# Splitting the expert weights of a mixture layer ahead of the expert loop, during an attention

## The chip, the cores and the metric

One core of a Trainium2 chip runs the whole program. The metric is the device time of one execution, in microseconds (us). PE is TensorE, VectorE stands in the profile as DVE, ScalarE as ACT, GpSimd as POOL, and SP is SyncE, whose queue issues every DMA of this kernel.

## What is computed

Two blocks on a tensor x of 2 x 1024 tokens by 128 features. Each block adds an attention and a feed-forward part to x. Cut to what matters:

```python
# block 0: cosine attention, 16 heads of 8, over 1024 tokens; and an FFN with FP4 (blockwise) quantised x, weights, hidden
xn = layernorm(x)
x = x + attn0(xn) + ffn0(xn)
# block 1: linear attention, 4 heads of 32; and a mixture of 160 experts, top 8, hidden size 64
xn = layernorm(x)
x = x + attn1(xn) + moe(xn)

def moe(x):
    probs = sigmoid(x @ router_w.T + expert_bias)
    combine = top8_normalised(probs) * 2.5                  # [tokens, 160], zero for experts not chosen
    h1 = silu(einsum('th,eih->eti', x, w_gate))             # w_gate [160, 64, 128]
    h1w = h1 * combine.T[:, :, None]
    routed = einsum('eti,ehi->th', h1w, w_down)             # w_down [160, 128, 64]
    return routed + silu(x @ w_gate_shared.T) @ w_down_shared.T
```

All experts are computed for all tokens.

## The kernel before

The program is written engine by engine, in one block per engine; each engine runs its own list in order, and semaphores (`wait_ge`, `then_inc`) tie the lists together. So an instruction that waits holds up everything behind it on its engine.

**Attention of block 0.** It runs twice, once for each batch of 1024 tokens (`attention(0)`, some 54 to 183 us, and `attention(1)`, some 211 to 340 us). Each has 64 steps (`STEPS0`) in 8 groups (`GRP`) of 8 steps (`NB`). A step on PE is `scores(st, 0)`, then `values(st - 2)`, then `scores(st, 1)`. `scores` is two matmuls into two PSUM banks of 0 to 3; ScalarE turns each set into exponentials `E` (L418, one instruction of 128 x 1024 for each `u`), and `values` is eight recorded matmuls (L1045) into bank 4 or 5. `scores(st + 1, 0)` waits until the exponential of `scores(st, 0)` has been taken, since both use the same banks. At a group's end VectorE copies the result to `OS` (L741, in `output(m)`), PE transposes it (`out_T(m)`, L1054, four transposes, at step 4 of the next group) into bank 6 or 7 in turn, and VectorE divides it (`divide(m)`, L728 and L733).

Between these, VectorE does other work in the order of its list. In the first attention: `second_heads(2)`, `output(0)`, `second_heads(3)`, `output(1)`, `quantise_weights()`, `output(2)`, then `quantise_x(g)` and `output(3 + g)` for g of 0 to 3, then the last `output`. In the second: `quantise_hidden(g)` and `output(8 + g)` for g of 0 to 3, then `residual()`, then the last four `output`. A quantisation is ten VectorE instructions, L646 to L666; `residual()` is two, L772 and L774.

**Expert loop.** 160 experts make 80 pairs (`NP`); a pair fills the 128 partitions. Each pair has 4 steps (`NC`), one for every 512 tokens, 320 in all. Weights and activations are used as a high and a low part in fp32r, so that a product is three matmuls of 128 x 512. A step on PE is `down(s)` (L1342 to L1344), then `gate(s + 4)` (L1335 to L1337). For a gate, ScalarE applies silu (L562), VectorE multiplies by the combine rows `CWB` (`weigh`, L936), ScalarE rounds to the high part (`high`, L358), and VectorE subtracts for the low part (`low`, L941); then the down matmuls follow.

Once per pair the raw weights, 64 KB of gate (`wg_raw`, L208) and 64 KB of down (`wd_raw`, L211), loaded by SP, are transposed by PE in `weights_T` (L1314, L1317) ahead of the gate of the next step; ScalarE makes the high parts (`w_high`), VectorE the low parts (`w_low`, L926). SP's order in the loop, for each pair: wait `wg_pe`, load gate; wait `m_dve`, load two combine rows for the first half of the tokens (L223); wait `wg_pe`, load down; wait `m_dve`, load two combine rows for the second half. A load of a combine row is 1024 values of one expert, broadcast from DRAM to 64 partitions, 256 KB written. Every buffer of weights and of combine rows is double, for even and odd pairs.

## Time and profile before

| | us |
|---|---|
| median of 3 runs | 920.35 |
| lowest, highest | 915.98, 921.47 |
| the profiled execution | 917.9 |
| its span | 915.7 |

| | busy us | share of the span |
|---|---|---|
| PE | 834.2 | 91% |
| PE weight loads | 524.2 | 57% |
| VectorE | 667.3 | 73% |
| ScalarE | 717.8 | 78% |
| GpSimd | 34.7 | 4% |

The span is the time from the first to the last instruction of the profiled execution. Busy times are averages over stages whose limits differ, so they say little alone; the stages are 0 to 54 us (loads, norms, heads), 54 to 183 (first attention), 183 to 211 (FFN of block 0), 211 to 340 (second attention), 340 to 418 (end of block 0, linear attention, routing), 418 to 909 (expert loop) and the output. A line of the chain or of a timeline gives start, duration and the instructions; in brackets stands how long the engine had been idle and what released it. A record of a matmul is a little longer than the distance to the next one, since matmuls are pipelined.

### The profile page before, as it was taken

Reading aid. Unit: us, or ns where it says so; the run is one execution under the profiler, and the core shown is the slowest. Engines: PE = TensorE matmul, PEld = TensorE weight load, DVE = VectorE, ACT = ScalarE, POOL = GpSimd, SP = SyncE. Lnnn points to the kernel's source line nnn. Section 1 sums busy time; section 2 is a strip of 40 time slices with the busy share of each in tenths; the row PEclk is TensorE's granted clock in tenths of the full one; section 3 lists DMA queues with packets and bytes.
Section 4 is the critical chain, followed back from the end, with each engine's and each line's share of the span. In section 5 each row is a group of like instructions: output and inputs, shape, how many; then the busy total and the mean of one; then the engine's idle time right before and its main releaser. Section 6 shows DMA issues by size and latency. Waiting matters only on the chain.

```text
span 915.7 us, 15851 instructions
## 1 busy us (share of the span) xinstructions
PE 834.2 (91%) x4516; PEld 524.2 (57%) x4516; DVE 667.3 (73%) x1358; ACT 717.8 (78%) x1263; POOL 34.7 (4%) x41
## 2 busy tenths in 40 slices
PE   4779989897999989897999999999999999999997
PEld 2421212171121229674777777777777777777775
DVE  5754734145683016973999999999999999999997
ACT  2779999857999985564888788877887778888886
POOL 1700000000000000400000000000000000000000
PEclk9969999998999999998999999999999999999999
DMA  4000000000000000006777777777877777777883
GB/s 117 1 1 1 1 1 1 1 1 0 1 1 1 1 1 2 12 30 175 188 199 197 192 200 195 195 198 191 204 194 192 194 193 195 195 199 194 199 201 96
DMA packets 66776, 99.88 MB, mean 109 GB/s; under 512 B 29270, under 2 KB 45942, under 8 KB 66742
## 3 DMA queue, kind: packets, MB, share of 16 engines
q1 hardware_dynamic: 66742, 99.44, 42.4%
q8 instruction: 20, 0.33, 0.1%
q14 instruction: 14, 0.11, 0.0%
HBM read 97.04 MB, written 2.36 MB: 109 GB/s over the span
## 4 chain that ended last, share of the span: by engine, by line
PE 48%; ACT 18%; DMA 11%; DVE 8%; issue 8%; SPq 5%; DVEq 1%; ACTq 0%
ACT E L418 15%; DMA wg_raw<-in_L_ffn_w_gate_dram 11%; PE PS L1335 6%; PE PS L1337 5%; PE PS L1336 5%; PE PS L1342 5%; PE PS L1344 5%; PE PS L1343 5%; PE PS L1045 4%; SPq L223 4%; PE PS L1030 2%; PE PS L1122 2%; DVE HM L936 2%; ACT SI L562 2%; PE PS L1314 1%
## 5 line engine op out<-in xcount | busy, mean ns | idle before, releaser
L562 ACT ACTIVATE SI<-PS 128x512 f32<-128x512 f32 x320 | 191.6, 599 | 86.9 <-PE PS L1337 86.7
L936 DVE TENSOR_TENSOR HM<-SI,CWB 128x512 f32<-128x512 f32 x320 | 221.5, 692 | 39.2 <-ACT SI L562 16.6
L418 ACT ACTIVATE E<-PS 128x1024 f32<-128x1024 f32 x256 | 241.6, 1024 | 8.7 <-PE PS L1030 7.4
L941 DVE TENSOR_TENSOR HLo<-HM,HH 128x512 fp32r<-128x512 f32 x320 | 219.1, 685 | 0.2
L358 ACT ACTIVATE HH<-HM 128x512 fp32r<-128x512 f32 x320 | 199.4, 623 | 3.7 <-DVE HM L936 3.7
L1045 PE MATMUL PS<-E,VS 128*32 128x512 f32 x1024 | 139.2, 616 | 0.4 <-ACT E L418 0.4
L1335 PE MATMUL PS<-XH,wgH 128*128 128x512 f32 x320 | 134.5, 420 | 0.0
L1342 PE MATMUL PS<-HH,wdH 128*128 128x512 f32 x320 | 128.4, 401 | 1.0 <-DVE HLo L941 1.0
L1344 PE MATMUL PS<-HH,wdL 128*128 128x512 f32 x320 | 127.1, 397 | 0.0
L1336 PE MATMUL PS<-XL,wgH 128*128 128x512 f32 x320 | 127.0, 397 | 0.0
L1337 PE MATMUL PS<-XH,wgL 128*128 128x512 f32 x320 | 126.8, 396 | 0.0
L1030 PE MATMUL PS<-QT,KT 32*128 32x512 f16 x512 | 97.9, 395 | 31.7 <-ACT E L418 23.7
L1343 PE MATMUL PS<-HLo,wdH 128*128 128x512 f32 x320 | 125.5, 392 | 0.0
L1030 PEld LDWEIGHTS PS<-QT,KT 32*128 32x128 f16 x512 | 23.9, 91 | 173.6 <-ACT E L418 168.2
L741 DVE COPY OS<-PS 128x512 f32<-128x512 f32 x16 | 11.1, 692 | 135.9 <-PE PS L1045 135.9
L1342 PEld LDWEIGHTS PS<-HH,wdH 128*128 128x128 f32 x320 | 60.5, 189 | 16.9 <-DVE HLo L941 2.5
L1344 PEld LDWEIGHTS PS<-HH,wdL 128*128 128x128 f32 x320 | 60.3, 188 | 15.4
L1337 PEld LDWEIGHTS PS<-XH,wgL 128*128 128x128 f32 x320 | 60.4, 189 | 14.5
L1343 PEld LDWEIGHTS PS<-HLo,wdH 128*128 128x128 f32 x320 | 60.5, 189 | 14.0
L1336 PEld LDWEIGHTS PS<-XL,wgH 128*128 128x128 f32 x320 | 60.8, 190 | 10.9
L1335 PEld LDWEIGHTS PS<-XH,wgH 128*128 128x128 f32 x320 | 60.5, 189 | 11.1 <-ACT SI L562 0.6
L1045 PEld LDWEIGHTS PS<-E,VS 128*32 128x32 f32 x1024 | 20.3, 109 | 31.6 <-issue 29.4
(214 smaller groups left out, 832.3 us busy)
## 6 DMA issues: line engine op xcount, KB each, us to landing
CWB<-combine_weights SPq DMA_DIRECT2D x320, 256.0 KB, 3.9
wg_raw<-in_L_ffn_w_gate_dram SPq DMA_DIRECT2D x80, 64.0 KB, 3.4
wd_raw<-in_L_ffn_w_down_dram SPq DMA_DIRECT2D x80, 64.0 KB, 3.7
X<-in_L_attn_x_dram SPq DMA_DIRECT2D x4, 256.0 KB, 3.8
combine_weights<-CWT SPq DMA_DIRECT2D x2, 512.0 KB, 2.9
out_dram<-X SPq DMA_DIRECT2D x4, 256.0 KB, 2.9
combine_weights<-CWT SPq DMA_DIRECT2D x2, 128.0 KB, 3.8
qkvw_raw<-in_L_attn_qkv_w_dram SPq DMA_DIRECT2D x1, 192.0 KB, 3.8
```

Of the source, the lines that this page charges most:

```text
L358: return nc.scalar.activation(dst, src, ACT.Copy)
L418: nc.scalar.activation(E[:, (2 * st + u) % NE_SLOTS, :], PS[:, 2 * u:2 * u + 2, :], ACT.Exp, scale=SCALE0).then_inc(S["exp_act"], 1)
L562: nc.scalar.activation(SI[:, slot % 2, :], bank(4 + slot % 2), ACT.Silu).then_inc(S["s_act"], 1)
L936: TT(HM[:, slot % 4, :], SI[:, slot % 2, :], CWB[:, q, half, CH * c:CH * c + CH], ALU.mult)\
L941: TT(HLo[:, slot % 4, :], HM[:, slot % 4, :], HH[:, slot % 4, :].bitcast(F32), ALU.subtract)\
L1045: last = MM(PS[32 * c:32 * c + 32, 4 + m % 2, :], VS[:, s, k, c, :], e, start=(k == 0), stop=(k == NB - 1), skip_group_check=True)
L1335: MM(o, wgH[:, q, :], XH[:, c], start=True, stop=False)
L1336: MM(o, wgH[:, q, :], XL[:, c], start=False, stop=False)
L1337: MM(o, wgL[:, q, :], XH[:, c], start=False, stop=True).then_inc(S["g_pe"], 1)
L1342: MM(o, wdH[:, q, :], HH[:, s, :], start=False, stop=False, skip_group_check=True)
L1343: MM(o, wdH[:, q, :], HLo[:, s, :], start=False, stop=False, skip_group_check=True)
L1344: MM(o, wdL[:, q, :], HH[:, s, :], start=False, stop=stop, skip_group_check=True)\
```

## The change

- The raw weights are loaded two pairs at a time, during the two runs of block 0's attention, into `WRAW` (two buffers); PE transposes the four tiles (gate and down of two pairs) into PSUM bank 7 (`transpose_weights(f)`), VectorE makes the high and the low part of all four in one copy and one subtract of 128 x 512 (`split_weights(f)`) into `WSPL` (two buffers), and SP stores them, 512 KB, to a DRAM tensor `w_dram`. There are 40 such fills: at every other step of `attention(0)` from step 32 (fills 0 to 15) and of `attention(1)` from its step 16 (fills 16 to 39), behind `scores(st, 1)`.
- The results of the attention (`out_T`, `divide`) use bank 6 alone, and `out_T(m)` waits for `divide(m - 1)`.
- On VectorE, `output(m)` becomes `group_end(m)`: the splits of that group's steps, then `output(m)`. `quantise_weights()` stands ahead of the second `output`, `quantise_x` and `quantise_hidden` run two at a time ahead of one `group_end`.
- In the expert loop the transposes, `w_high` and `w_low` are gone. SP loads the split gate weights (128 KB, 1 KB a partition) once the four gate groups of the pair before in that buffer are done, and the split down weights (128 KB) once its four down groups are done; the down load now stands last in SP's order for a pair. PE waits for the gate load ahead of a pair's first gate and for the down load ahead of its first down.

```diff
         def load_gate(eng, j, q):
-            eng.dma_start(wg_raw[:, q, :], one(eg_v, j, "o p h -> (o p) h")).then_inc(S[f"wgl{q}"], 16)
+            eng.dma_start(WG[:, q, :, :].bitcast(F32), one(w_dram[:, 0], j, "o p l c -> (o p) l c")).then_inc(S[f"wgl{q}"], 16)
 
         def load_down(eng, j, q):
-            eng.dma_start(wd_raw[:, q, :].rearrange("p (e i) -> p e i", e=2),
-                          one(ed_v, j, "o h e i -> (o h) e i")).then_inc(S[f"wdl{q}"], 16)
+            eng.dma_start(WD[:, q, :, :].bitcast(F32), one(w_dram[:, 1], j, "o p l c -> (o p) l c")).then_inc(S[f"wdl{q}"], 16)
+        NF = NP // 2
+        FILLS0 = 16
+        def fill_at(b, st):
+            first = 32 if b == 0 else 16
+            return None if st < first or st % 2 else FILLS0 * b + (st - first) // 2
...
+            def load_raw(f):
+                pr = slice(2 * f, 2 * f + 2)
+                sp.dma_start(WRAW[:, f % 2, :, 0, :], eg_v[pr].rearrange("j p h -> p j h")).then_inc(S[f"wr{f % 2}"], 16)
+                for k in range(2):
+                    sp.dma_start(WRAW[:, f % 2, k, 1, :].rearrange("p (e i) -> p e i", e=2), ed_v[2 * f + k])\
+                      .then_inc(S[f"wr{f % 2}"], 16)
+            for f in range(2):
+                load_raw(f)
+            for f in range(NF):
+                sp.wait_ge(S["ws_dve"], f + 1)
+                sp.dma_start(w_dram[2 * f:2 * f + 2].rearrange("j g p l c -> p j g l c"), WSPL[:, f % 2].bitcast(F32))\
+                  .then_inc(S[f"wst{f % 2}"], 16)
+                if f + 2 < NF:
+                    load_raw(f + 2)
             sp.wait_ge(S["x1_dve"], NT)
+            for f in range(2):
+                sp.wait_ge(S[f"wst{f}"], 16 * (NF // 2))
...
                     j = i * 2 + (2 + q)
-                    sp.wait_ge(S["wg_pe"], i * 2 + (1 + q))
+                    sp.wait_ge(S["g_pe"], i * STEPS + (NC * q + NC))
                     load_gate(sp, j, q)
                     sp.wait_ge(S["m_dve"], i * STEPS + (NC * q + NC // 2))
                     load_combine(sp, j, q, 0)
-                    sp.wait_ge(S["wg_pe"], i * 2 + (2 + q))
-                    load_down(sp, j, q)
                     sp.wait_ge(S["m_dve"], i * STEPS + (NC * q + NC))
                     load_combine(sp, j, q, 1)
+                    sp.wait_ge(S["d_pe"], i * STEPS + (NC * q + NC))
+                    load_down(sp, j, q)
...
+            def split_weights(f):
+                dve.wait_ge(S["wT2_pe"], f + 1)
+                if f >= 2:
+                    dve.wait_ge(S[f"wst{f % 2}"], 16 * (f // 2))
+                src = bank(7).rearrange("p (j g c) -> p j g c", j=2, g=2)
+                hi, lo = WSPL[:, f % 2, :, :, 0, :], WSPL[:, f % 2, :, :, 1, :]
+                nc.vector.tensor_copy(hi, src)
+                dve.drain()
+                TT(lo, src, hi.bitcast(F32), ALU.subtract).then_inc(S["ws_dve"], 1)
+
+            def group_end(m):
+                for st in range(m % GRP * NB, m % GRP * NB + NB):
+                    if fill_at(m // GRP, st) is not None:
+                        split_weights(fill_at(m // GRP, st))
+                output(m)
+
             second_heads(2)
-            output(0)
+            group_end(0)
             second_heads(3)
-            output(1)
             quantise_weights()
-            output(2)
-            for g in range(NG):
-                quantise_x(g)
-                output(3 + g)
-            for m in range(3 + NG, GRP):
-                output(m)
+            group_end(1)
+            quantise_x(0)
+            quantise_x(1)
+            group_end(2)
+            quantise_x(2)
+            quantise_x(3)
+            for m in range(3, GRP):
+                group_end(m)
...
-            for g in range(NG):
-                quantise_hidden(g)
-                output(GRP + g)
+            quantise_hidden(0)
+            quantise_hidden(1)
+            group_end(GRP)
+            quantise_hidden(2)
+            quantise_hidden(3)
+            group_end(GRP + 1)
             residual()
-            for m in range(GRP + NG, 2 * GRP):
-                output(m)
+            for m in range(GRP + 2, 2 * GRP):
+                group_end(m)
...
             def out_T(m):
                 pe.wait_ge(S["oc_dve"], m + 1)
-                if m >= 2:
-                    pe.wait_ge(S["ao_dve"], m - 1)
+                if m >= 1:
+                    pe.wait_ge(S["ao_dve"], m)
                 for j in range(GT):
-                    last = TR(bank(6 + m % 2)[:, P * j:P * j + P], OS[:, m % 2, P * j:P * j + P], ident[:, :])
+                    last = TR(bank(6)[:, P * j:P * j + P], OS[:, m % 2, P * j:P * j + P], ident[:, :])
                 last.then_inc(S["oT_pe"], 1)
+
+            def transpose_weights(f):
+                pe.wait_ge(S[f"wr{f % 2}"], 48 * (f // 2 + 1))
+                if f >= 1:
+                    pe.wait_ge(S["ws_dve"], f)
+                for k in range(2):
+                    for w in range(2):
+                        at = P * (2 * k + w)
+                        last = TR(bank(7)[:, at:at + P], WRAW[:, f % 2, k, w, :], ident[:, :])
+                last.then_inc(S["wT2_pe"], 1)
...
                     scores(st, 1)
+                    f = fill_at(b, st - st0)
+                    if f is not None:
+                        transpose_weights(f)
                     if st % NB == LAG + 2 and st > st0 + NB:
                         out_T(st // NB - 1)
...
             def expert_steps(i, last):
                 for s in range(STEPS):
                     q, c = s // NC, s % NC
-                    if c == 0:
-
-                        pe.wait_ge(S["wgl_dve"], i * 2 + (2 + q))
-                    down(s, i * STEPS + s, q, last and q == 1)
-                    if c == 0 and not (last and q == 1):
-                        weights_T(None if last else q, 1 - q, (i * 16 + 32, i * 16 + 16 * (1 + q)), q)
+                    down(s, i * STEPS + s, q, last and q == 1, i * 16 + 16 if c == 0 else None)
                     if not (last and s + AHEAD >= STEPS):
-                        gate(s + AHEAD, i * STEPS + (s + AHEAD - 1), (s + AHEAD) // NC % 2)
+                        n = s + AHEAD
+                        gate(n, i * STEPS + (n - 1), n // NC % 2, i * 16 + 16 * (1 + n // STEPS) if c == 0 else None)
```

## Rows read from the trace of the kernel before

**Rows 1.** Windows: length; busy us of PE, PEld, DVE, ACT, POOL; clock, DMA share, GB/s.

```profile
212.00:340.00 128.00, 113.58 (x796) 25.34 (x796) 56.03 (x65) 121.87 (x132) 0.80 (x2) 0.97 0.00 1
500.00:600.00 100.00, 98.58 (x435) 77.30 (x435) 93.00 (x167) 80.83 (x168) 0.00 (x0) 1.00 0.77 196
```

**Rows 2.** Timeline of ScalarE, second attention: start us, us, instructions.

```profile
218.49 20.94 ACT L418 ACTIVATE E<-PS 128x1024 f32<-128x1024 f32 x22 [1.33 <-PE PS L1030]
239.72 15.17 ACT L418 ACTIVATE E<-PS 128x1024 f32<-128x1024 f32 x16 [0.29 <-PE PS L1030]
```

**Rows 3.** Timeline of PE: first attention, then second.

```profile
94.83 0.66 PE L1054 MATMUL PS<-ident,OS 128*128 128x128 f32 x4
...
237.32 0.66 PE L1054 MATMUL PS<-ident,OS 128*128 128x128 f32 x4
...
237.91 0.39 PE L1030 MATMUL PS<-QT,KT 32*128 32x512 f16 x2
...
241.71 0.39 PE L1030 MATMUL PS<-QT,KT 32*128 32x512 f16 x2 [0.52 <-ACT E L418]
...
247.66 1.07 PE L1045 MATMUL PS<-E,VS 128*32 128x512 f32 x8
...
249.31 0.39 PE L1030 MATMUL PS<-QT,KT 32*128 32x512 f16 x2 [0.26 <-ACT E L418]
```

**Rows 4.** Timeline of PE in the expert loop, without waits.

```profile
509.57 0.40 PE L1336 MATMUL PS<-XL,wgH 128*128 128x512 f32 x1
...
513.76 0.40 PE L1336 MATMUL PS<-XL,wgH 128*128 128x512 f32 x1
```

**Rows 5.** Source views: first down matmul (ns min/median/max); idle before gate transposes (us, times).

```profile
L1342 PE MATMUL PS<-HH,wdH x320: 392/397/628, 422.3 to 908.0; 128*128 128x512 f32 x160
...
  DMA wg_raw<-in_L_ffn_w_gate_dram: 43.3, 72
```

**Rows 6.** DMA issues (KB each, median us to landing); source view of the down load.

```profile
combine_weights<-CWT SPq DMA_DIRECT2D x2, 512.0 KB, 2.9
...
L211 SPq DMA_DIRECT2D wd_raw<-in_L_ffn_w_down_dram x80: 433/530/545, 371.0 to 893.6; - x80
...
DMA to landing us min/median/max: 1.9/3.7/7.7
```

**Rows 7.** Timeline of VectorE, start of the expert loop.

```profile
426.18 0.69 DVE L941 TENSOR_TENSOR HLo<-HM,HH 128x512 fp32r<-128x512 f32 x1
```

**Rows 8.** Windows at the start of the expert loop.

```profile
420.00:426.00 6.00, 2.66 (x10) 1.46 (x9) 2.42 (x4) 2.72 (x5) 0.00 (x0) 1.00 1.03 242
430.00:436.00 6.00, 6.00 (x20) 4.71 (x19) 3.25 (x6) 3.35 (x6) 0.00 (x0) 0.67 0.33 87
```

**Rows 9.** Timeline of VectorE, first attention.

```profile
81.79 0.36 DVE L713 COPY K<-HL 128x256 f16<-128x256 f16 x2
...
90.15 1.20 DVE L646 TENSOR_REDUCE qs<-gu_raw 88x64 f32<-88x1024 f32 x1
...
103.44 0.53 DVE L666 TENSOR_TENSOR dn_raw<-qy,qs 128x352 f32<-128x352 f32 x1
```

**Rows 10.** Timeline of VectorE, second attention.

```profile
210.54 1.62 DVE L646 TENSOR_REDUCE qs<-HF 128x88 f32<-128x1408 f32 x1
...
220.62 1.63 DVE L666 TENSOR_TENSOR HF<-qy,qs 128x1408 f32<-128x1408 f32 x1
...
277.88 0.69 DVE L741 COPY OS<-PS 128x512 f32<-128x512 f32 x1 [2.44 <-PE PS L1045]
...
279.20 2.29 DVE L772 TENSOR_TENSOR X<-X,XN 128x2048 f32<-128x2048 f32 x1
...
281.56 2.29 DVE L774 TENSOR_TENSOR X<-X,outb 128x2048 f32<-128x2048 f32 x1
```

**Rows 11.** Timeline at the end of the first attention.

```profile
181.84 0.66 PE L1054 MATMUL PS<-ident,OS 128*128 128x128 f32 x4 [0.82 <-DVE OS L741]
...
182.03 0.29 DVE L733 TENSOR_TENSOR AO<-PS,rden 128x128 f32<-128x128 f32 x1
```

More of the change, by code:

```diff
@@ L143, in two_block_layer_kernel @@
         aoT = sb("aoT", [P, 2, P], F32, ph0)
+        WRAW = sb("WRAW", [P, 2, 2, 2, P], F32, ph0)
+        WSPL = sb("WSPL", [P, 2, 2, 2, 2, P], F32R, ph0)
         ph0.close()
@@ L170, in two_block_layer_kernel @@
         SHS = sb("SHS", [P, 2, CH], F32, ph1)
[L171 to L176 removed]
+        WG = sb("WG", [P, 2, 2, P], F32R, ph1)
+        WD = sb("WD", [P, 2, 2, P], F32R, ph1)
         SI = sb("SI", [P, 2, CH], F32, ph1)
@@ L191, in two_block_layer_kernel @@
             "k_pe km_dve ek_act q_pe q_act v_pe v_act ekT_pe ekT_act cx_pe cx_dve mix_pe mix_dve "
-            "sh_pe sh_act hmask_pool res_pool cws0 cws1 cwl00 cwl01 cwl10 cwl11 wgl0 wgl1 wdl0 wdl1 wg_pe wgh_act wgl_dve "
+            "sh_pe sh_act hmask_pool res_pool cws0 cws1 cwl00 cwl01 cwl10 cwl11 wgl0 wgl1 wdl0 wdl1 wr0 wr1 wT2_pe ws_dve wst0 wst1 "
             "g_pe d_pe s_act m_dve hi_act lo_dve mt_act fo_pe fo_dve stored"
@@ L198, in two_block_layer_kernel @@
         cw_dram = nc.dram_tensor("combine_weights", [NE, T], F32).ap()
+        w_dram = nc.dram_tensor("split_weights", [NP, 2, P, 2, P], F32).ap()
         block = es.enter_context(nc.Block())
@@ L550, in _ @@
             by_expert(7)
-            def w_high(n, what, q, at_bank):
-                act.wait_ge(S["wg_pe"], n)
-                for dst, at in what:
-                    last = copy(dst[:, q[at], :], bank(6 + at_bank)[:, P * at:P * at + P])
-                last.then_inc(S["wgh_act"], 1)
             def silu(slot, count):
@@ L582, in expert_steps @@
                         high(s + AHEAD - 2, i * STEPS + (s + AHEAD - 2))
-                    q = s // NC
-                    if s % NC == 0 and not (last and q == 1):
-                        what = ((wdH, 1),) if last else ((wgH, 0), (wdH, 1))
-                        w_high(i * 2 + (3 + q), what, (q, 1 - q), q)
             with act.Fori(0, NP // 2 - 1) as i:
@@ L726, in divide @@
                 dve.wait_ge(S["oT_pe"], m + 1)
-                src = bank(6 + m % 2).rearrange("p (t c w) -> p (t c) w", t=GT, c=HG)
+                src = bank(6).rearrange("p (t c w) -> p (t c) w", t=GT, c=HG)
                 nc.vector.reciprocal(rden[:, m % 2, :], src[:, :, HD0])
@@ L920, in _ @@
             choose(7)
-            def w_low(n, what, q, at_bank):
-                dve.wait_ge(S["wgh_act"], n)
-                for dst, hi, at in what:
-                    last = TT(dst[:, q[at], :], bank(6 + at_bank)[:, P * at:P * at + P], hi[:, q[at], :].bitcast(F32),
-                              ALU.subtract)
-                last.then_inc(S["wgl_dve"], 1)
             def weigh(slot, count, loaded):
@@ L957, in expert_steps @@
                         low(s + AHEAD - 2, i * STEPS + (s + AHEAD - 2))
-                    q = s // NC
-                    if s % NC == 0 and not (last and q == 1):
-                        what = ((wdL, wdH, 1),) if last else ((wgL, wgH, 0), (wdL, wdH, 1))
-                        w_low(i * 2 + (3 + q), what, (q, 1 - q), q)
             with dve.Fori(0, NP // 2 - 1) as i:
@@ L1305, in _ @@
             combine_T(7)
-            def weights_T(gate_q, down_q, loads, at_bank):
-                gate_n, down_n = loads
-                last = None
-                o = bank(6 + at_bank)
-                if gate_q is not None:
-                    pe.wait_ge(S[f"wgl{gate_q}"], gate_n)
-                    last = TR(o[:, 0:P], wg_raw[:, gate_q, :], ident[:, :])
-                if down_q is not None:
-                    pe.wait_ge(S[f"wdl{down_q}"], down_n)
-                    last = TR(o[:, P:2 * P], wd_raw[:, down_q, :], ident[:, :])
-                last.then_inc(S["wg_pe"], 1)
-            weights_T(0, 0, (16, 16), 0)
             for c in range(NC):
```

35 lines of the change are left out of this document (13 added, 22 removed).

## The prediction

> **What bounds the kernel now.** Read first the windows by stage, for which engine is full in which stretch. In the second attention ScalarE is busy 121.87 of 128 us and the DMA moves nothing; in the expert loop PE is busy 98.58 of 100, VectorE 93.00, ScalarE 80.83, with the DMA at 0.77 and 196 GB/s [rows 1]. So the two stages have different limits, and the change takes work out of the second and puts it into the first.
>
> In attention, ScalarE's timeline gives the pace: 16 exponentials take 15.17 us, 0.948 each, and eight steps cost 15.17 plus one idle of 0.29 [rows 2], 1.93 a step. The reader should see what the 0.29 is: PE put four transposes (`out_T`) into a step, 0.59 us from 237.32 to 237.91, and the next scores came late [rows 3]. Two steps later PE again waited for ScalarE, 0.52 before 241.71. PE work is thus close to ScalarE's: values 1.07 by their record, two sets of scores of 0.39, each overlapping the next by some 0.07, about 1.64 a step.
>
> In the loop, PE's timeline gives 1.397 us a step where nothing is waited for (509.57 to 513.76, three steps) [rows 4]. The source view of the first down matmul gives 422.3 to 908.0 for 319 steps, 1.523 on average, and that of the gate weights' transpose shows why: 43.3 us of waiting for the raw gate weights, in 72 of 80 pairs [rows 5]. Some of it is the weight-load side waiting while a matmul still runs, so it isn't all span; the rest of the gap is the 160 transposes.
>
> **What the change gives in the loop.** It removes the transposes from PE, two copies per pair from ScalarE and two subtracts from VectorE; neither of those engines bounds. The waits for gate weights should go as well: the gate load may start when the four gate groups of the pair that used its buffer are done, and its data are needed five steps later (7.0 us less one gate group, 6.3), while the down load of half its size lands in 3.7 us by the median and in 1.9 on a nearly idle queue [rows 6]. The down load now comes last in SP's order and waits for `d_pe`; behind it stand the next pair's gate and combine loads. The combine load of the next half starts a little later than it could (by 1.5 us at most, SP being held until `d_pe`) and is needed more than 6 us after its issue.
>
> Start: the first down is where it was, 422.3. The second needs `HLo`, which exists at 426.18 + 0.69 = 426.9, because VectorE waits for combine rows and no edit touches these [rows 7]. From the second to the last down there are 318 steps: 318 x 1.397 = 444.2, less 3 gaps without a gate group (3 x 0.70) = 442.1, so the last down starts at 869.0 instead of 908.0: 39.0 us gained. PE now idles over 3 us before 426.9, longer before; at 430 to 436 the granted clock was 0.67 [rows 8], that is largely the lower of its levels, 1.2 GHz. If it falls again, some 12 matmuls cost 0.2 us more each, 2.7 us at most. I take **38 us**.
>
> **What it costs in the attentions.** 40 fills of two pairs: 16 in the first attention from step 32, 24 in the second from step 16, one every other step.
>
> (a) *Moved quantisation, first attention.* `quantise_weights` now stands ahead of `output(1)`. `second_heads(3)` ends at 82.15, the block takes 13.82 (90.15 to 103.97), the copy 0.69 [rows 9, 10]: `OS` is there at 96.7. PE ran this `out_T` at 94.83 [rows 3]. **1.9 us**.
>
> (b) *Moved quantisation, second attention.* This is the large one. VectorE starts at 210.54; one hidden quantisation takes 11.7 (to 222.25). The new order is two of them, a copy (0.7), two more, a copy with `divide` (1.3), the residual (279.20 to 283.85, 4.65), and only then the first weight split of this attention, fill 16 [rows 10]. 210.54 + 46.8 + 0.3 (drains) + 0.7 + 1.3 + 4.65 = 264.3, and a split is a copy and a subtract of 128x512 from PSUM, 0.69 + 0.08 + 0.69 by the `OS` copy's row: 265.8. PE, however, wants fill 17 at local step 18 and waits there for `ws_dve` >= 17. That step's values start at 247.66, and the next scores ran at 249.31 [rows 3]. Behind the waiting transposes stand all scores, so ScalarE runs dry. With the burst the next scores come at 266.4: 17.1 late. Before, VectorE's late copies delayed nobody; now PE waits for it in its own queue. **17 us**. PE then restarts after 16 us of idleness. At this attention's own start, ScalarE waited 1.33 us in its first steps [rows 2]; I add **1.3**. The Trainium skill (TensorE: Matmul & The Clock Gate, section "What's actually happening") says that an idle array falls to half rate; the row of the loop's start at 0.67 agrees.
>
> (c) *The bursts.* PE's work in two steps with a burst is 2 x 1.64 + 0.59 = 3.87, ScalarE's 4 x 0.948 = 3.79. A lone burst costs 0.29; one that follows by two steps falls where PE had 0.52 to spare, perhaps nothing. Between 0 and 0.29 I take 0.15 for 30 fills (4.5) and 0.29 for the 10 that share a step with an `out_T` (2.9). The single bank brings a handover too: at a group's end VectorE does `output` first (1.3 to its next work), then the split of the fill before (1.46), 2.8 after the values; PE wants the next fill one step and a set of scores later, 2.2. 0.6 late, at 9 group ends: 5.4. Together **12.8**, from 0 to 20.
>
> (d) *The single bank 6.* The last `out_T` of each attention now waits for `divide` (182.03 + 0.29) instead of starting at 181.84 [rows 11]: 2 x 0.55 = **1.1**.
>
> (e) *The transfers.* Per fill SP issues one 512 KB store and three loads of 256 KB together. In a queue so far empty (share 0.00 [rows 1]) that is 0.79 MB in 3.87 us, 203 GB/s, below the 242 that the queue held [rows 8]. From burst to raw data of the fill after next: transposes, handover and split 2.2, four issues by SP at 0.53 each 2.1, landing 1.9 on an empty queue, up to 2.9 behind a store of this size [rows 6]: 6.2 to 7.2 against 7.7 between those bursts. Hidden, with little to spare. Six more loads at the very start lie behind all others: nothing.
>
> Sum: -38 + 1.9 + 17 + 1.3 + 12.8 + 1.1 = -3.9. The profiled execution took 917.9 (span 915.7), 2.45 below the median of 920.35. 917.9 - 3.9 = 914.0, and against the median **916.4 us**.
>
> **The rivals.**
> *The loop becomes DMA-bound (slower).* Bytes per pair rise from 1.18 to 1.31 MB, the time per pair should fall from 6.1 to 5.59: 235 GB/s asked. The most that the queue held with combine rows waiting was 242, at share 1.03 [rows 8]: 5.42 us a pair, only 0.17 inside the limit. It decides from 235 down. Were 225 all it gives, a pair takes 5.83 and the loop 19 us more: 935. For it: the small margin, taken at one place. Against: a quarter of a load's rows are longer now (1 KB for 256 and 512 B). The Trainium skill (DMA: Bandwidth & Descriptors, section "Specifications") gives 358 GB/s of HBM per core; an estimate by that page is 3.7 us a pair and no such bound. The trace doesn't show that rate held over microseconds.
> *The transfers of the fills come late.* If stores beside loads take 2 us longer than (e), each second fill waits; a wait of 0.4 at every fill is 16 us: 932.
> *The bursts fit.* If PE keeps up in (c) and only part of the handovers show, the cost is 2 instead of 12.8: 905.5. For it: the 0.52. Against: 3.87 over 3.79.
> *The change works as its parts say and PE's wait in (b) isn't there* (VectorE much earlier than its rows): 18.3 less, 898. Only a wrong reading of the order gives this.
>
> **How the numbers follow.** Forecast case 45% (909 to 925), bursts fit 23%, DMA-bound loop 15%, late fills 10%, no wait in (b) 4%, the rest something dearer. The range takes 901 to 936. One per cent is 9 us, about what a measurement of this kernel tells apart. Faster by more (under 911): nearly all of two cases and the low edge of the forecast, 0.29. Slower (over 929.5): 0.24. Within: 0.47.
>
> **What would show it.** Right: a PE wait of about 17 us for VectorE in the second attention at the new transposes; ScalarE idle in the attentions up by some 30; `OS` copies of the second attention's first two groups at about 234 and 258; no PE wait for weights in the loop, 5.59 us a pair, DMA share near 0.9. Wrong: the loop at 5.8 a pair or more with PE waiting for `WG`, `WD` or, through ScalarE, for `CWB`; PE waiting for `WRAW`; a second attention of about 135 us, which would take (b) away.

## The result, and the profile after

| | before | changed |
|---|---|---|
| time, median | 918.66 us | 929.16 us |
| range, executions | 914.14 to 921.47, 19 | 921.17 to 964.20, 19 |
| ratio to before | | 1.0098, 95% interval 1.0076 to 1.0120 |

The change makes the kernel 1% slower. A slightly faster one was forecast, 914.0 for a profiled execution of 917.9 before (916.4 against a median of 920.35). The executions spread far more than those of the kernel before. The one that was profiled took 964.20 (span 962.0) and is the slowest of them; a second profiled one of the same code, `after_asis5` below, took 931.67 (span 929.5) and is near the median. Both are used, each for what it shows. The ratio leaves out the seven executions of the changed kernel that lie more than 1.5% above its fastest.

First the end and the start of the loop, in the source view of the first down matmul, which answers [rows 5]. Changed kernel, the 962.0 us execution (ns min/median/max, first and last start):

```profile
L1361 PE MATMUL PS<-HH,WD x320: 388/401/632, 468.4 to 954.3; 128*128 128x512 f32 x160
```

The same view of the execution of 929.5 us:

```profile
L1361 PE MATMUL PS<-HH,WD x320: 388/398/628, 466.1 to 921.8; 128*128 128x512 f32 x160
```

The loop starts 46.1 and 43.8 us later than before (422.3); 34.1 was forecast. It then takes 485.9 us in the one, no less than the 485.7 before, and 455.7 in the other; 447.7 was forecast.

Windows of the changed kernel (962.0), with the columns of [rows 1]:

```profile
212.00:340.00 128.00, 100.21 (x660) 30.29 (x658) 79.32 (x96) 93.17 (x102) 0.81 (x2) 0.89 0.32 90
...
520.00:560.00 40.00, 40.00 (x174) 32.28 (x173) 36.92 (x59) 32.03 (x58) 0.00 (x0) 1.00 1.01 226
560.00:600.00 40.00, 39.78 (x159) 28.20 (x157) 33.01 (x53) 30.04 (x53) 0.00 (x0) 1.00 1.07 211
600.00:640.00 40.00, 39.59 (x156) 27.72 (x156) 32.11 (x52) 29.54 (x52) 0.00 (x0) 1.00 1.06 212
```

In the second attention ScalarE, the pace-setter, is down from 121.87 to 93.17 us of work in 128. In the loop PE starts 174 matmuls in 40 us up to 560; then the DMA share rises from 1.01 to 1.07, the rate falls from 226 to 211 GB/s and PE to some 157. It stays so to the end. Of the waits of the same execution, those that bear on this (us, times, longest):

```profile
DVE HM L959 <- DMA CWB<-combine_weights: 85.3, 65, 10.3
...
ACT E L442 <- PE PS L1047: 48.7, 61, 16.7
...
PE PS L1081 <- DVE WSPL L809: 24.5, 10, 16.3
```

ScalarE's idle time before the exponentials (L442) is 48.7 us; the loop's wait is VectorE's for the combine rows. And PE's timeline in the second attention, the place of term (b):

```profile
257.27 0.66 PE L1081 MATMUL PS<-ident,WRAW 128*128 128x128 f32 x4
277.46 1.09 PE L1081 MATMUL PS<-ident,WRAW 128*128 128x128 f32 x4 [16.32 <-DVE WSPL L809]
```

### The profile page after: what moved, and what is told of

It reads as the page before. It is cut to its first block, busy times and chain, and to the rows that moved or that the text cites. A ratio compares the mean times of both kernels' runs of the same rounds, so it can differ in the third digit from the quotient of the medians.

```text
span 962.0 us, 15734 instructions
## 1 busy us (share of the span) xinstructions
PE 867.5 (90%) x4516; PEld 518.1 (54%) x4516; DVE 677.4 (70%) x1278; ACT 697.0 (72%) x1103; POOL 35.3 (4%) x41
## 4 chain that ended last, share of the span: by engine, by line
PE 64%; DVE 14%; ACT 6%; DMA 5%; issue 4%; DVEq 3%; SPq 3%; ACTq 0%
PE PS L1361 10%; PE PS L1352 8%; PE PS L1363 7%; PE PS L1353 7%; PE PS L1362 7%; PE PS L1354 7%; ACT E L442 5%; PE PS L1062 5%; PE PS L1047 2%; DMA WRAW<-in_L_ffn_w_down_dram 2%; PE PS L1152 2%; DMA CWB<-combine_weights 2%; PE PS L1081 1%; SPq L282 1%; DVE OS L751 1%
## 5 line engine op out<-in xcount | busy, mean ns | idle before, releaser
L442 ACT ACTIVATE E<-PS 128x1024 f32<-128x1024 f32 x256 | 244.1, 1025 | 49.5 <-PE PS L1047 48.7
L1361 PE MATMUL PS<-HH,WD 128*128 128x512 f32 x320 | 140.5, 439 | 6.6 <-DVE HLo L964 4.8
L1352 PE MATMUL PS<-XH,WG 128*128 128x512 f32 x320 | 133.2, 416 | 0.0
L1353 PE MATMUL PS<-XL,WG 128*128 128x512 f32 x320 | 127.0, 397 | 0.0
L1354 PE MATMUL PS<-XH,WG 128*128 128x512 f32 x320 | 126.5, 395 | 0.0
L1363 PE MATMUL PS<-HH,WD 128*128 128x512 f32 x320 | 126.5, 395 | 0.0
L1362 PE MATMUL PS<-HLo,WD 128*128 128x512 f32 x320 | 125.9, 393 | 0.0
L1361 PEld LDWEIGHTS PS<-HH,WD 128*128 128x128 f32 x320 | 60.1, 188 | 63.6 <-DVE HLo L964 31.3
L807 DVE CAST WSPL<-PS 128x512 fp32r<-128x512 f32 x40 | 27.6, 689 | 71.1 <-PE PS L1081 71.1
L1352 PEld LDWEIGHTS PS<-XH,WG 128*128 128x128 f32 x320 | 60.1, 188 | 31.8 <-ACT SI L579 10.3
L1354 PEld LDWEIGHTS PS<-XH,WG 128*128 128x128 f32 x320 | 60.4, 189 | 14.7
L1363 PEld LDWEIGHTS PS<-HH,WD 128*128 128x128 f32 x320 | 60.2, 188 | 14.7
L1353 PEld LDWEIGHTS PS<-XL,WG 128*128 128x128 f32 x320 | 60.4, 189 | 11.6 <-issue 0.2
L1362 PEld LDWEIGHTS PS<-HLo,WD 128*128 128x128 f32 x320 | 60.5, 189 | 8.4
L1081 PE MATMUL PS<-ident,WRAW 128*128 128x128 f32 x160 | 26.9, 292 | 30.4 <-DVE WSPL L809 24.5
```

The source lines that it names most:

```text
L442: nc.scalar.activation(E[:, (2 * st + u) % NE_SLOTS, :], PS[:, 2 * u:2 * u + 2, :], ACT.Exp, scale=SCALE0).then_inc(S["exp_act"], 1)
L1352: MM(o, WG[:, q, 0, :], XH[:, c], start=True, stop=False)
L1353: MM(o, WG[:, q, 0, :], XL[:, c], start=False, stop=False)
L1354: MM(o, WG[:, q, 1, :], XH[:, c], start=False, stop=True).then_inc(S["g_pe"], 1)
L1361: MM(o, WD[:, q, 0, :], HH[:, s, :], start=False, stop=False, skip_group_check=True)
L1362: MM(o, WD[:, q, 0, :], HLo[:, s, :], start=False, stop=False, skip_group_check=True)
```

## The experiments

Labels that begin with "after" are the changed kernel, with an edit where one is shown; ratios are to runs of the kernel before on the same chip (medians 917.2 to 918.8). Two questions: what made the attentions dearer than 34.1 us, and why the loop lost part, or all, of its gain.

### The stall of 16 us: `after_spread`

```diff
-            quantise_hidden(0)
-            quantise_hidden(1)
-            group_end(GRP)
-            quantise_hidden(2)
-            quantise_hidden(3)
-            group_end(GRP + 1)
-            residual()
+            quantise_hidden(0)
+            group_end(GRP)
+            quantise_hidden(1)
+            group_end(GRP + 1)
+            pieces.extend(hidden_pieces(2) + hidden_pieces(3))
...
                         split_weights(fill_at(m // GRP, st))
+                        if pieces:
+                            dve.drain()
+                            pieces.pop(0)()
```

> The changed kernel, but in the second attention the third and fourth hidden quantisation and the residual are cut into their 22 instructions, one behind each weight split, instead of running in a block ahead of the first. Theory (PE waits 16 to 17 us for the first split, then restarts at the lower clock): the wait goes, ScalarE's idle before exponentials falls from 50 to some 32 us, the first down matmul comes 17 to 18 us sooner, at about 450, and the time is 909 to 911. Rival (the wait is replaced: each piece holds up the split behind it): 4 us or more come back at the 6 group ends. Second rival (the loop is DMA-bound and gives back what is gained ahead of it): would be seen as a longer loop; not expected, since the loop's loads do not start earlier relative to its work.

Its first down matmul started at 450.6, against 468.4, 467.0 and 466.1 in the three profiled executions of the changed kernel, so 15.5 to 17.8 sooner. (Five more profiles below are of kernels that leave the attentions as they are; there it starts at 466.4 to 470.3.) The source view of its weight transposes says that the long wait is gone:

```profile
L1107 PE MATMUL PS<-ident,WRAW x160: 272/273/333, 121.6 to 361.7; 128*128 128x128 f32 x160
its engine sat idle before it (us, times) until:
  DVE WSPL L830: 9.0, 10
  DMA WRAW<-in_L_ffn_w_down_dram: 9.0, 10
```

Ten waits for VectorE of 0.90 each are left (24.5 us before, with one of 16.3), and ten for the raw weights, 9.0 us (5.9 before, in the view below). The loop took 454.3. Whole times: 914.82, 932.5, 941.28 and 912.76, all above the 909 to 911 that were expected and too far apart for a verdict; the first down matmul is the sound reading here.

### Raw loads ahead of the store: `after_loads_first`

```diff
                 sp.wait_ge(S["ws_dve"], f + 1)
+                if f + 2 < NF:
+                    load_raw(f + 2)
                 sp.dma_start(w_dram[2 * f:2 * f + 2].rearrange("j g p l c -> p j g l c"), WSPL[:, f % 2].bitcast(F32))\
...
-                if f + 2 < NF:
-                    load_raw(f + 2)
```

> The changed kernel with SP issuing the three raw loads of fill f + 2 ahead of the store of fill f, not behind it. Theory L (the raw loads come late behind the store): PE's waits for WRAW in the attentions vanish, ScalarE's idle time before the exponentials falls from 50 to about 40 us, first down matmul near 460. Rival (those waits only take the place of waits for the split, so nothing is won): the waits move to the split or to the exponentials, first down still 465 to 468.

The one execution took 928.3; the first down matmul started at 459.0, 7.1 to 9.4 sooner. Source view of its weight transposes, then of the changed kernel's (962.0):

```profile
L1081 PE MATMUL PS<-ident,WRAW x160: 272/273/449, 120.7 to 370.5; 128*128 128x128 f32 x160
its engine sat idle before it (us, times) until:
  DVE WSPL L809: 24.3, 10
```

```profile
L1081 PE MATMUL PS<-ident,WRAW x160: 272/273/473, 120.8 to 379.8; 128*128 128x128 f32 x160
its engine sat idle before it (us, times) until:
  DVE WSPL L809: 24.5, 10
  DMA WRAW<-in_L_ffn_w_down_dram: 5.9, 9
```

The raw weights' waits are gone and the others are the same. Ahead of the store, a raw load of down weights lands in 2.1 us by the median, behind it in 2.9. The 5.9 us of waits cost more than themselves, 7 to 9 us; ScalarE's idle time before the exponentials falls by 8.4 as well (48.7 to 40.3 us). This is one execution, beside three of the changed kernel. Why they were late, the changed kernel's timelines show. VectorE, PE and SP around a group's end:

```profile
157.48 0.69 DVE L751 COPY OS<-PS 128x512 f32<-128x512 f32 x1 [3.96 <-PE PS L1062]
158.09 0.25 DVE L738 RECIPROCAL rden<-PS 128x16 f32<-128x16 f32 x1
158.41 0.29 DVE L743 TENSOR_TENSOR AO<-PS,rden 128x128 f32<-128x128 f32 x1
158.62 0.68 DVE L807 CAST WSPL<-PS 128x512 fp32r<-128x512 f32 x1
159.37 0.69 DVE L809 TENSOR_TENSOR WSPL<-PS,WSPL 128x512 fp32r<-128x512 f32 x1
```

```profile
155.44 0.66 PE L1081 MATMUL PS<-ident,WRAW 128*128 128x128 f32 x4
160.21 0.63 PE L1081 MATMUL PS<-ident,WRAW 128*128 128x128 f32 x4 [0.90 <-DVE WSPL L809]
164.49 0.66 PE L1081 MATMUL PS<-ident,WRAW 128*128 128x128 f32 x4 [0.44 <-DMA WRAW<-in_L_ffn_w_down_dram]
```

```profile
160.09 0.38 SPq L289 DMA_DIRECT2D split_weights<-WSPL  x1
160.52 0.51 SPq L280 DMA_DIRECT2D WRAW<-in_L_ffn_w_gate_dram  x1
161.07 1.57 SPq L282 DMA_DIRECT2D WRAW<-in_L_ffn_w_down_dram  x2
```

The burst of 155.44 is split only after the group's `output`: done at 160.06, 4.6 us after the burst and not 2.2. SP needs to 162.6 for the store and the three loads that stand behind that split, and the burst that wants their data is due at 164.05. In `after_asis5` these waits are 0.33 to 0.59 a group, and 1.60 and 1.75 in the last two.

### How long the split holds the bank: `after_turned`

This one has the spreading, the loads first, and two more edits. The scratch holds the transposed weights once, unsplit; the loop splits them as the kernel before did. Its combine loads stand where they stood before, with the gate load of the next pair behind the down load.

```diff
-                nc.vector.tensor_copy(hi, src)
-                dve.drain()
-                TT(lo, src, hi.bitcast(F32), ALU.subtract).then_inc(S["ws_dve"], 1)
+                nc.vector.tensor_copy(WTR[:, f % 2], src).then_inc(S["ws_dve"], 1)
...
+                    sp.wait_ge(S["wgl_dve"], i * 2 + (2 + q))
+                    load_down(sp, j, q)
+                    load_gate(sp, i * 2 + (3 + q), 1 - q)
```

> From the changed kernel with all three repairs: the scratch holds the turned weights once, as f32, not split. VectorE's work for a fill is one copy (0.69 us) instead of a copy and a subtract (1.46), the store is 256 KB; in the loop ScalarE and VectorE split the loaded weights as in the kernel before, PE has no transposes, and a pair loads 1.18 MB into raw buffers that come free a pair earlier. If the handover of the single bank costs 0.9 us at each group's end because the split is long, it falls to about 0.1: first down matmul at 434 to 437 (442.6 with the split), loop 450, 893 to 896 us in all. Rival: the bursts themselves are the cost (1.37 us a group stays), first down 441 to 443, 899 to 902. Rival D: the loop now has VectorE (three 128x512 operations a step and two small ones a pair) as its bound, pair period over 5.65 us, over 903.

896.17 us, ratio 0.9757 (0.9724 to 0.9790), within the forecast, and the fastest kernel of this study. The `OS` copies that end the groups of the first attention give the price of a fill:

```profile
123.39 0.69 DVE L778 COPY OS<-PS 128x512 f32<-128x512 f32 x1 [2.96 <-PE PS L1124]
139.54 0.69 DVE L778 COPY OS<-PS 128x512 f32<-128x512 f32 x1 [4.72 <-PE PS L1124]
155.70 0.69 DVE L778 COPY OS<-PS 128x512 f32<-128x512 f32 x1 [4.72 <-PE PS L1124]
```

A group takes 16.15 or 16.16 us here, 15.46 in the kernel before, 16.83 in `after_loads_first` and 17.30 to 17.34 in the changed kernel. So the four bursts of a group cost 0.69, the handover of a long split 0.68 and the late raw loads about 0.5 (the 0.68 includes whatever the store of half the size gives). PE's waits for VectorE at the transposes, ten of 0.90, are gone. The first down matmul starts at 435.5, the last at 884.9: a loop of 449.4, at 211 GB/s and 0.84 of DMA share between 500 and 600. VectorE, at 96.59 us in 100, didn't become its bound: PE was busy 100.00.

### Fewer bytes in the loop: `after_half_combine` and `after_light`

`after_half_combine` loads only half of the columns in each combine load of the loop (1.311 MB a pair become 0.786):

```diff
-                    load_combine(sp, j, q, 0)
+                    load_half(sp, j, q, 0)
...
-                    load_combine(sp, j, q, 1)
+                    load_half(sp, j, q, 1)
```

> The changed kernel with the four combine loads of a pair cut to half their columns in the loop (0.79 MB a pair instead of 1.31, same number of issues and of waits; the other half of each row keeps old weights, which leaves part of the load out). If the queue is what holds the loop back (theories Q and B): 5.52 us a pair, 441 to 443 us from first to last down, no waits for WG, WD or CWB, 918 to 920 us in all. Rival C (the loop's extra time is in reading the split weights, their longer landing, or in the engines themselves): the loop stays at 450 us or more, over 926.

`after_light` loads only the high part of the split weights (1.180 MB a pair), same issues otherwise:

```diff
-                    load_gate(sp, j, q)
+                    load_high(sp, j, q, 0, WG, "wgl")
...
-                    load_down(sp, j, q)
+                    load_high(sp, j, q, 1, WD, "wdl")
```

> Leaves out, in the expert loop, the low halves of the split weights: they are loaded for the first two pairs only, so a pair moves 1.18 MB as in the kernel before, and PE, VectorE and ScalarE do all their work (with stale low parts). Theory A (DMA queue bounds the loop): PE's waits for WG, WD and VectorE's for CWB go, first to last down takes 442 to 446 us, the runs lie close together, and the time is 920 to 922, some 6 below the changed kernel's. Theory B (the loop is not the matter): within 1 us of the changed kernel, same spread between runs.

With 0.786 MB: first and last down 466.4 and 916.3, a loop of 449.9, no wait for `CWB`, `WG` or `WD` among the largest; 925.87 us, executions 925.63 to 928.44, where 918 to 920 was expected. The loop is as long as rival C put it (450 or more), but not for its reason: from 500 to 600 us PE is busy 100.00, at 1.397 us a step as in the kernel before, with the split weights read as in the changed kernel. So the queue is what lengthens the loop beyond this, and 449.9 is PE's own length, not 441 to 443. The difference lies at its two ends. PE's timeline and windows at the start:

```profile
466.44 0.50 PE L1368 MATMUL PS<-HH,WD 128*128 128x512 f32 x1 [0.91 <-DVE HLo L971]
...
471.68 0.50 PE L1368 MATMUL PS<-HH,WD 128*128 128x512 f32 x1 [3.57 <-DVE HLo L971]
```

```profile
472.00:478.00 6.00, 6.00 (x21) 4.71 (x20) 4.58 (x8) 3.32 (x7) 0.00 (x0) 0.72 0.14 50
```

5.2 us to the second down, and the clock at 0.72, so the lower level in part of these 6 us, after the wait of 3.57. From the second down to the last it is 444.6 us, 2.5 over the 442.1 of the prediction. Of these, 1.65 are the steps right behind the wait: the downs start at 471.68, 473.31, 475.87 and 477.52, three steps in 5.84 us for 4.19. The other 0.9 is at the end, where the last downs start at 911.88, 913.28, 914.06, 915.46 and 916.26: three steps without a gate group save 1.2 us, not 3 x 0.70. The gap and the lower clock stand in the prediction; my expectation of this run had forgotten them.

With 1.180 MB the forecast of 920 to 922 missed: 928.46 (1.0126, 1.0075 to 1.0178), loop 453.0. Its rate fell, too, where the share went over 1:

```profile
600.00:640.00 40.00, 40.00 (x173) 32.30 (x172) 37.12 (x58) 31.89 (x58) 0.00 (x0) 1.00 0.90 211
...
760.00:800.00 40.00, 40.00 (x170) 30.93 (x169) 35.29 (x57) 31.21 (x57) 0.00 (x0) 1.00 1.06 207
```

211 GB/s at 0.90, then 207 at 1.06, with the same loads. `after_turned` moves the same bytes at 0.84 to the end, but its four combine loads of a pair go out in twos 2.1 us apart; here they follow each other after 0.66. So a limit in bytes alone isn't the cause.

### How the loads are bunched: `after_even`, `after_even5`, `after_asis5`, `after_again`

SP's issues in the loop of the changed kernel (962.0):

```profile
523.76 0.34 SPq L210 DMA_DIRECT2D WD<-split_weights  x1
524.48 0.33 SPq L207 DMA_DIRECT2D WG<-split_weights  x1
525.07 2.46 SPq L229 DMA_DIRECT2D CWB<-combine_weights  x4
529.35 0.34 SPq L210 DMA_DIRECT2D WD<-split_weights  x1
```

All four combine loads of a pair, 1 MB, stand behind the waits for `d_pe` and `g_pe` and come in one row; then SP is idle. In the kernel before they came in twos. `after_even` holds each for one weighing more:

```diff
-                    sp.wait_ge(S["m_dve"], i * STEPS + (NC * q + NC // 2))
+                    sp.wait_ge(S["m_dve"], i * STEPS + (NC * q + NC // 2 + 1))
                     load_combine(sp, j, q, 0)
-                    sp.wait_ge(S["m_dve"], i * STEPS + (NC * q + NC))
+                    sp.wait_ge(S["m_dve"], i * STEPS + (NC * q + NC + 1))
```

How little this moves, SP's issues in `after_even` show:

```profile
523.88 0.33 SPq L207 DMA_DIRECT2D WG<-split_weights  x1
524.47 3.37 SPq L229 DMA_DIRECT2D CWB<-combine_weights  x4
```

The four still stand in one row with the gate load, over 3.37 us instead of 2.46: the third starts 1.1 or 1.6 us behind the second instead of 0.66 (2.1 in the kernel before).

> The changed kernel with one edit in the loop: each combine load is held for one weighing more (m_dve one higher), so that SP no longer issues the down load, the gate load and all four combine loads in one row and then nothing; same bytes (1.31 MB a pair). Theory Q (the queue holds the rate only while it isn't kept full by loads bunched behind one wait): the loop stays at 5.52 us a pair, 442 to 447 us from first to last down matmul, no drop of the rate behind 560 us, about 919 us in all. Rival B (1.31 MB in 5.5 us is beyond the queue, however the loads are ordered): the rate drops as before, loop 453 us or more, 926 us or more. Rival W (holding the loads a step longer makes them late): waits for CWB from the first pairs on, over 935.

> The kernel of after_even once more, beside the unchanged one of the next run and in more executions. Theory Q (bunched loads fill the queue): all its executions lie in 925 to 932, the unchanged kernel's own in 921 to 950, with a third of them over 932. Rival B (only the bytes count): both spread alike.

> The changed kernel as it is, beside after_even5. Both theories: median 927 to 931, single executions up to 950 or 964, where the rate in the loop has fallen to 212 to 217 GB/s and 1.06 of share. Theory Q says that after_even5 doesn't do so, rival B that it does as often.

> The changed kernel once more, for a second profile. Theory A (the loop is bound by the DMA queue, and how far depends on what rate the queue happens to hold in the run): the rate in the loop differs from the first profile's 212 GB/s, the loop's length goes with it (1.31 MB a pair: at 225 GB/s 5.8 us a pair, at 235 5.6), and the attentions are as before, the first down matmul again at about 468. Theory B (the loop keeps PE's pace and the time lies in the attentions alone): first down matmul well off 468, the loop at 5.6 us a pair as in the others.

`after_again` and `after_asis5` are the changed kernel without an edit. Windows of `after_even`, then of `after_asis5`:

```profile
500.00:600.00 100.00, 100.00 (x431) 80.70 (x430) 92.63 (x144) 80.18 (x144) 0.00 (x0) 1.00 0.97 234
```

```profile
500.00:600.00 100.00, 99.82 (x426) 78.79 (x426) 91.03 (x143) 79.22 (x143) 0.00 (x0) 1.00 1.05 233
```

The same bytes: spaced loads keep the share at 0.97 and PE full, bunched ones bring 1.05 and a landing of 6.0 us for a combine load instead of 4.4. The loop: 449.9 and 451.2 in the two spaced profiles; 485.9, 475.0 (`after_again`, 951.84 us) and 455.7 in the three of the changed kernel. In `after_again` the rate fell too, to 216 to 219 GB/s, and its loop lies between the other two, as its theory A said. Single executions: spaced 925.88, 927.44, 928.85, 929.4, 930.88, 931.39, 931.4, 931.58; unchanged, beside the second four of these, 927.1, 931.43, 931.67, 939.7, 950.33, 957.67, and of the 19 of the table eight are over 932. The median of those six, 935.68, is above my 927 to 931, since half of them are in the tail. The medians with spaced loads, 928.42 and 931.13, are not clearly below 929.16, and the 919 of theory Q was missed by 9 us. What spacing takes away is the tail: none of eight over 932, as the expectation of `after_even5` had it, against 11 of 25. That is few executions, and it isn't a cure: one of four of `after_all`, below, which is spaced too, took 929.05 against 900.44 to 902.7.

### What the queue gives: `after_wide`

Each combine load of the loop a quarter wider, 1.573 MB a pair.

```diff
-                    load_combine(sp, j, q, 0)
+                    load_wide(sp, j, q, 0)
```

> The changed kernel with each combine load of the loop made a quarter wider (320 KB instead of 256; the added columns are not used), 1.573 MB a pair instead of 1.311, same issues and waits. It measures what the queue gives once it is never empty. If that is 212 to 217 GB/s as in the disturbed loop: 7.25 to 7.42 us a pair, loop 580 to 594 us, some 1055 to 1070 in all. If it is 236 to 250 (the best stretches): 6.3 to 6.7 a pair, loop 504 to 533, 980 to 1010.

Two executions, 1014.05 (profiled) and 996.24. A window of the profiled one (233 GB/s from 800 to 900 us):

```profile
500.00:600.00 100.00, 89.65 (x354) 63.49 (x354) 72.73 (x117) 67.70 (x117) 0.00 (x0) 1.00 1.04 231
```

The loop took 537.0 us, 6.71 a pair, 234 GB/s. If the other differs by its loop alone, that is 519 us and 242 GB/s. The first is just outside the faster of my two cases (504 to 533), the second in it. PE's pace in the changed kernel asks for 1.311 MB in 5.59 us: 235. In the profiled execution there is no margin, in the other it would be 3%.

This is the rate of the loop's mix of loads and not of the queue as such. In the changed kernel's first attention, where stores and raw loads run and no combine rows, the same full share carries more:

```profile
144.00:148.00 4.00, 3.61 (x30) 1.29 (x22) 1.13 (x3) 3.71 (x4) 0.00 (x0) 1.00 1.01 294
```

### All repairs, and none of the change: `after_all`, `before_gate_early`

`after_all` is the spreading, the loads first and the even spacing together.

```diff
+                if f + 2 < NF:
+                    load_raw(f + 2)
...
-                    sp.wait_ge(S["m_dve"], i * STEPS + (NC * q + NC))
+                    sp.wait_ge(S["m_dve"], i * STEPS + (NC * q + NC + 1))
```

> The changed kernel with all three repairs: hidden quantisation spread behind the splits, raw loads ahead of the store, combine loads of the loop spaced. Theory Q and L: first down matmul near 444 (450.6 with the spreading alone), loop 442 to 445, 895 to 899 us in all, about that of the kernel before with the gate load early. Rival B: first down as there, loop 454 with a drop of the rate, 908 to 912.

`before_gate_early` is the kernel before, with each raw gate load issued right behind the down load of the pair before it, not a wait later:

```diff
-                    sp.wait_ge(S["wg_pe"], i * 2 + (1 + q))
-                    load_gate(sp, j, q)
...
                     sp.wait_ge(S["wg_pe"], i * 2 + (2 + q))
                     load_down(sp, j, q)
+                    if not (last and q == 1):
+                        load_gate(sp, i * 2 + (3 + q), 1 - q)
```

> The kernel before, with one edit in SP's order: the gate load of the next pair is issued right behind the down load, ahead of the wait for the second half's combine rows, about 3 us earlier than now. No fills, no splits in DRAM. Theory (gate waits come from the place of the load in SP's order): the 43 us of waits for wg_raw go, a pair takes 4 x 1.397 + 0.23 = 5.82 us, first to last down 461 instead of 486, total 893 to 896. Rival (the loads are late because the queue is full, share 0.77): the waits shrink by less than half, total above 905.

`after_all`: 902.59 us, 0.9823 (0.9793 to 0.9853); first down 442.6, near the 444 expected; the loop 450.2, not 442 to 445, for the start that I had forgotten here too, and so the time is over 895 to 899. Against `after_loads_first` (459.0) the spreading brings the first down matmul 16.4 sooner. `before_gate_early`: 901.02, 0.9818 (0.9790 to 0.9847), where 893 to 896 was expected. Its loop takes 467.8, expected 461; PE's timeline holds no wait at the pair's turn, but the two transposes delay the next matmuls by 0.21:

```profile
603.64 0.39 PE L1350 MATMUL PS<-HH,wdL 128*128 128x512 f32 x1
603.88 0.27 PE L1320 MATMUL PS<-ident,wg_raw 128*128 128x128 f32 x1
603.98 0.27 PE L1323 MATMUL PS<-ident,wd_raw 128*128 128x128 f32 x1
604.01 0.47 PE L1341 MATMUL PS<-XH,wgH 128*128 128x512 f32 x1
604.32 0.39 PE L1342 MATMUL PS<-XL,wgH 128*128 128x512 f32 x1
```

From the last down to the second gate matmul, 603.64 to 604.32, it is 0.68 us, where two distances of 0.233 would do without the transposes. 80 times 0.21 is 16.8, of the 17.9 between 467.8 and 449.9; the rest is at the start, where the second down comes 7.70 us after the first, for 5.24. Of the 35.8 us that the loop could gain (485.7 - 449.9), half was a late load, to be had for a few moved lines, and only the other half needed the transposes out of the loop.

## Why the prediction was wrong

I forecast a small gain and the change costs 1%. Against the execution near the median, `after_asis5` (931.67), it is 17.7 us over the 914.0 forecast. The loop's start came at 466.1 instead of 422.3 + 34.1 = 456.4, 9.7 late; the loop took 455.7 instead of 447.7, 8.0 long.

**The loop's gain** (38 forecast). PE's own gain was 35.8, as `after_half_combine` shows. The pace of 1.397 us a step was right. The gap before the second down was 5.2 and not 4.6; the clock, which I had weighed at 2.7 and then taken off at 1.0, cost 1.65; and the steps without a gate group at the end save 1.2 and not 2.1. Together that is 2.2 of the 8.0.

**The DMA-bound loop**, the rival with 15%, is the other 5.8, and up to 36 in the profiled execution. The step that failed is the 242 GB/s that the queue "held": it came from one window of 6 us [rows 8]. The profiled execution of `after_wide` holds 231 to 234 over 500 us; its other one would come to 242, so that 242 can be had, but not counted on. I compared two rates and never asked in what row SP would issue the loads; bunched, they cost share (1.05 for 0.97) and landing time at the same rate. The Trainium skill (DMA: Bandwidth & Descriptors, section "Specifications") gives 358 GB/s of HBM per core. The profiled loops carried at most 237 in windows of 40 us (`after_even`), and the stretch of stores and raw loads shown above 294; the measurement decides. What brings the rate from 226 down to 211 within one execution, and in some executions only, isn't settled: spacing makes it rarer, far fewer bytes (`after_half_combine`) leave no sign of it, somewhat fewer (`after_light`) do. It was not tried whether loads issued from another queue change it.

**(b) The stall** (17 and 1.3 forecast). Right in place, cause and size: PE waited 16.32 us for VectorE at fill 17, and undoing it gave back 15.5 to 17.8, or 16.4 by `after_all` and `after_loads_first`, whose attentions differ in this alone. Behind it the granted clock read 0.50, the lower level, after 16.3 us without a matmul:

```profile
276.00:280.00 4.00, 2.54 (x14) 1.02 (x14) 2.58 (x4) 0.82 (x1) 0.00 (x0) 0.50 0.44 129
```

(This is the changed kernel's window, in the execution of 962.0 us.) The Trainium skill (TensorE: Matmul & The Clock Gate, section "What's actually happening") gives an idle array 1.2 GHz, half of 2.4. The trace agrees.

**(c) The bursts** (12.8 forecast, or 1.28 a group). `after_loads_first` shows 1.37 a group: 0.69 of bursts, for 0.74 (three at 0.15 and one at 0.29), and 0.68 of handover, for 0.6. The rival that the bursts fit is ruled out, and so is the one without a wait in (b).

**(e) The transfers** (nothing forecast, late fills as a rival with 10%). This is the failed step of the attentions: 7.1 us. I counted 2.2 us from a burst to its split and 7.7 to the burst that wants the data. That holds inside a group. At a group's end the split stands behind `output` and came after 4.6, by my own figures of (c), which I hadn't carried over to (e). What is then left, 4 us, had to hold four issues by SP and a landing. The rival put 0.4 at every fill; it was about 0.5 once a group, and more in the last two groups (1.60 and 1.75 in `after_asis5`, 1.00 and 1.81 in the execution of 962.0 us).

**(a) and (d).** (d) stands: the last `out_T` of the first attention waits 1.44 us for `divide`, where it waited 0.82 for the copy. (a) is right up to the `OS` copy of `output(1)`, which starts at 95.92, against 96.0 by my sum. But with the single bank 6 `out_T(1)` waits for `divide(0)` as well, which I had charged only to the last `out_T`:

```profile
97.28 0.63 PE L1071 MATMUL PS<-ident,OS 128*128 128x128 f32 x4 [2.37 <-DVE AO L743]
```

That is 2.45 later than the 94.83 before, for 1.9 forecast.

**A term that I put at nothing: the clock between the attentions.** The attentions without late transfers cost 36.7 us (459.0 - 422.3) for 34.1 forecast. Of the 2.6, some 1.5 lie behind the last `out_T` of the first attention. The window of the changed kernel (962.0) there:

```profile
196.00:200.00 4.00, 4.00 (x25) 3.47 (x24) 2.67 (x5) 1.56 (x3) 0.00 (x0) 0.75 0.00 0
```

Before it PE had been idle for 1.44 and 0.76 us. In `after_loads_first` it is the same (0.74 from 194 to 198 us), and the 16 transposes of `Hn` there take 3.58 us; in `after_turned`, at a clock of 1.00 after the same two gaps, they take 2.10. Why it fell in one and not in the other is open. The rest of the 2.6 is (a) and the dearer handovers of (c).

Net: 7.1 (raw loads) + 2.6 (clock, (a) and (c)) + 2.2 (both ends of the loop) + 5.8 (queue) = 17.7. The dear terms were named, each with its place, and (b), the largest, was right. Two things that I had only as rivals, late fills and a DMA-bound loop, each came true in part, in the same executions, and no term came out cheaper by as much. The time lies inside the 901 to 936 because the range was wide enough for either rival, and not because the sum held.

## What to carry to other kernels

- Before work is moved out of a loop to save a wait, try to issue the load that is waited for earlier: here that alone gave 1.8% (901.0 us), while the whole change cost 1%.
- A margin in a queue's rate has to be read over the whole stage and together with the order of its issues: all loads behind one wait make a burst, and within some percent of the limit single executions fall off, here by up to 4% (964.20 against a median of 929.16).
- When a step is inserted before an event (a group's end), every chain through it, that of the next transfer too, has to be timed at that event and not in the middle of a group.

## What the runs showed of the hardware

- With 1.311 MB a pair and PE busy throughout, the DMA queue carried 229 to 237 GB/s in the loop (`after_even`), and mostly less once its share stood at 1.04 to 1.07: 211 to 213 GB/s in the profiled execution of the changed kernel, 216 to 219 in `after_again`, 228 in `after_spread`, 206 or 207 in `after_light`, but 230 to 234 in `after_wide`. The level differs between executions of the same code. Stores and raw loads without combine rows reached 294 at 1.01.
- The change in rate comes in the middle of the loop, without a change in the work (between 520 and 600 us above), and lasts to the end in the two slowest; in `after_loads_first` the rate went from 222 back to 236.
- Two transposes of 128x128, 0.27 us each by their rows, delay the matmul stream by only 0.21 together (`before_gate_early`).
- After a wait of 3.57 us the clock read 0.72 over 6 us and three steps cost 1.65 us more (`after_half_combine`); after gaps of 1.44 and 0.76 us it read 0.82 and 0.75 in the changed kernel and 1.00 in `after_turned`.
